# A fused transformer tower on one core: the token chain's last norm applied on ScalarE instead of VectorE

## The chip, the core and the metric

One core of a Trainium2 chip runs the whole program. The metric is the device time in microseconds of one execution; lower is better. Five engines work from queues of their own, each in program order, and wait for each other through semaphores: TensorE (PE, its weight loads shown as PEld), VectorE (DVE), ScalarE (ACT), GpSimd (POOL) and SyncE (SP, which only issues transfers).

## What is computed

The input `x` holds 64 images of 128 tokens by 64 x 3 values. Three blocks follow one another; cut to what matters:

```python
# tokens: three convolutions over a (token, column) grid with layer norms between
h = relu(conv1(layernorm(x)))
h = relu(conv2(layernorm(h)))
h = relu(conv3(layernorm(h)))            # 2 x 128 channels
res = concat(h[:, :128], h[:, 128:])     # rows of 2J = 128 values
res = layernorm(res, ln1_g, ln1_b)       # the norm of this change
h = res @ out_w + out_b
# attention with L1 distances, 8 heads of 64 values, both directions
n = layernorm(h)
a[s, t] = softmax(-sum_w |q[s, w] - k[t, w]| / 8)   # with one zero logit more
h = h + n + (gated a @ vf + a' @ vb) @ fanin_w + fanin_b
# an expert of 32 for each row
h = h + relu(relu(layernorm(h) @ W1[i]) @ W2[i])
```

A layer norm is `(x - mean) * rstd`, then a gain and a bias. For `res`, gain and bias are applied later, when the transposed rows are copied (L613), so the norm of this change is only `(x - mean) * rstd`.

## The kernel before

**Pairs and slots.** Images go in pairs: 32 pairs, `iteration(i)` for each. An iteration has 128 slots (`SLOTS`). Each slot has one `unit`: TensorE makes, with 4 matmuls at L387, the differences q - k of one head, 16 query tokens and all 128 keys, in one of three places of `psU` (slot modulo 3). Then either VectorE sums their absolute values (L788, called D units here, 71 of 128 slots) or ScalarE takes the absolute values (L587, A units, the 57 slots that `shared` names). A units are summed further by GpSimd: a transfer that adds one half to the other (`first_add`, L1045), two additions (`tree`, L1056 and L1060), and last VectorE (`last_adds`, L799, 17 slots after the group's end). TensorE may fill a place only after the unit three slots earlier was read.

**The work between the units.** Around the units each engine runs the rest of the tower at slots written out by hand: attention of the second image of the pair before, the experts of the pair before, the norm of the next pair, and the token chain `tok` of pair i + 2. `TOK_AT` gives the chain's slots: copy 3, norm a 9, conv1 20 to 42, norm b 43, conv2 53 to 65, norm c 67, conv3 75 to 109, norm d 110, transpose `turn` 121, `out` 126. `gap` = 7: a norm's statistics are taken at its slot, the norm is applied 7 slots on. A slot's extra work stands behind that slot's unit in an engine's queue.

**The last norm (d).** Slot 109: ScalarE's two ReLUs (L609). Slot 110: VectorE takes the statistics `std` and `mvd` (L813, L818), GpSimd computes `ved` = variance + eps (L1072) and `rstdd` = `ved` to the power -1/2 (L1074) in `root`, behind its `first_add` of slot 110. Slot 117: VectorE waits for `rstdd` and writes `resn` for both images (L861, two instructions), behind D unit 117. Slot 121: TensorE waits for it and transposes (L427). Slot 122: ScalarE copies with gain and bias (L613).

Around slot 117 the units are: A 115, D 116, D 117, A 118, D 119, A 120, D 121, A 122, D 123, A 124, D 125 to 127. TensorE has the attention's 16 matmuls at L486 in slots 113 to 119. Slots 119 to 122 also hold `last_adds` of slot 102 (L799), the sum L891, ScalarE's `o_half` (L707) and `th` (L712), and the gate L896.

The other norms that ScalarE applies (`norm` at L624, `experts` at L718) already use the form of the change: a scale `rstd` and a bias `nmr` = -mean x rstd, which GpSimd makes in `shift` (L1079 and L1081). Semaphore counts of each engine follow the lists of names `TOK_PE`, `TOK_ACT`, `TOK_DVE`, `TOK_POOL`.

Before the iterations, a prologue runs the token chains of pairs 0 and 1 with no units beside them; the last two iterations have no token chain. So 30 of 32 chains run beside units.

Of the kernel before, what the change touches and what calls it, by code (L numbers as in the profile page):

```python
# [21 lines left out]
ALU = mybir.AluOpType  # L22
ACT = mybir.ActivationFunctionType
AX = mybir.AxisListType

T = 128
J = 64
# [54 lines left out]


TOK_PE = Steps("conv1 conv2 conv3 turn out")
TOK_ACT = Steps("copy relu1 relu2 relu3a relu3b turned")
LN = "stat{0}0 stat{0}1 wait{0} aggr{0}0 aggr{0}1 "
LN_APPLY = "gain{0}0 gain{0}1 shift{0}0 shift{0}1 "
TOK_DVE = Steps("".join(LN.format(x) + LN_APPLY.format(x) for x in "abc") + LN.format("d") + "norm0 norm1 h")
TOK_POOL = Steps("vara rstda varb rstdb varc rstdc vard rstdd")

NORM_DVE = Steps("stat0 stat1 wait aggr0 aggr1")
NORM_POOL = Steps("var rstd mean shift hx")
# [24 lines left out]
def spread(slot, at, length, count):  # L117
# [14 lines left out]
TOK_AT = dict(copy=3, a=9, conv1=20, len1=22, b=43, conv2=53, len2=12, c=67, conv3=75, len3=34, d=110, turn=121,  # L132
              out=126, root=0, gap=7)


def vit_tower(nc, a, out):
# [4 lines left out]
    with ExitStack() as ctx:  # L141
        def sb(name, shape, dt=F32):
            return ctx.enter_context(nc.sbuf_tensor(name, shape, dt))
# [39 lines left out]
        resn = sb("resn", [T, 2, 2 * J])  # L183
        resT = sb("resT", [T, 2, T])
        st = {k: sb("st" + k, [T, 2, 6]) for k in "abcdne"}
        mv = {k: sb("mv" + k, [T, 2, 2]) for k in "abcdne"}
        ve = {k: sb("ve" + k, [T, 2]) for k in "abcdne"}
        rstd = {k: sb("rstd" + k, [T, 2]) for k in "abcdne"}
        mr = {k: sb("mr" + k, [T, 2]) for k in "ne"}
        nmr = {k: sb("nmr" + k, [T, 2]) for k in "ne"}  # L190
        h = sb("h", [T, 2, LAT])

        x1 = sb("x1", [T, 2, LAT])
# [40 lines left out]
        psC = ctx.enter_context(nc.psum_tensor("psC", [T, 512], F32))  # L234
# [116 lines left out]
        def _(pe):  # L351
# [39 lines left out]
            def tok(p, slot):  # L391
                for n in spread(slot, TOK_AT["conv1"], TOK_AT["len1"], 15):
                    dy, m = n // 3, n % 3
                    dx, o, w0, wn = ((1, 0, 0, 3), (0, 1, 0, 2), (2, 0, 1, 2))[m]
                    if n == 0:
                        pe.wait_ge(tok_dve, TOK_DVE.after(p, "shifta1"))
                        if not (isinstance(p, int) and p == 0):
                            pe.wait_ge(tok_dve, TOK_DVE.after(p - 1, "h"))
                    o_v = psC[:, 0:6 * J].rearrange("p (b j w) -> p b j w", b=2, w=3)
                    mm = nc.tensor.matmul(o_v[:, :, :, o:o + wn], w1[:, 3 * dy + dx, :],  # L400
                                          c1in[:, :, dy:dy + J, w0:w0 + wn], start=(n == 0), stop=(n == 14))
                    if n == 14:
                        mm.then_inc(tok_pe, 1)
                for n in spread(slot, TOK_AT["conv2"], TOK_AT["len2"], 10):
                    if n == 0:
                                                pe.wait_ge(tok_dve, TOK_DVE.after(p, "shiftb1"))
                    dy, dx = n // 2, n % 2
                    mm = nc.tensor.matmul(psC[:, 0:4 * J].rearrange("p (b j w) -> p b j w", b=2, w=2),  # L408
                                          w2[:, n, :], c2in[:, :, dy:dy + J, dx:dx + 2],
                                          start=(n == 0), stop=(n == 9))  # L410
                    if n == 9:
                        mm.then_inc(tok_pe, 1)
                for n in spread(slot, TOK_AT["conv3"], TOK_AT["len3"], 20):
                    if n == 0:
                        pe.wait_ge(tok_act, TOK_ACT.after(p, "relu2"))
                        pe.wait_ge(tok_dve, TOK_DVE.after(p, "shiftc1"))
                    hf, m = n // 10, n % 10
                    dy, dx = m // 2, m % 2
                    mm = nc.tensor.matmul(psC[:, 0:2 * T].rearrange("p (b a j) -> p b a j", b=2, a=2)[:, :, hf, :],  # L419
                                          w3[:, m, hf * T:hf * T + T], c3in[:, :, dy:dy + J, dx],  # L420
                                          start=(m == 0), stop=(m == 9))
                    if n == 19:
                        mm.then_inc(tok_pe, 1)
                if slot == TOK_AT["turn"]:
                    pe.wait_ge(tok_dve, TOK_DVE.after(p, "norm1"))
                    for b in range(2):
                        mm = nc.tensor.transpose(psC[:, b * T:b * T + T], resn[:, b, :], ident[:, :])  # L427
                    mm.then_inc(tok_pe, 1)
                if slot == TOK_AT["out"]:
                    pe.wait_ge(tok_act, TOK_ACT.after(p, "turned"))  # L430
                    for b in range(2):
                        mm = nc.tensor.matmul(psC[:, b * LAT:b * LAT + LAT], resT[:, b, :], wout[:, :],
                                              start=True, stop=True)
                    mm.then_inc(tok_pe, 1)
# [142 lines left out]
        def _(act):  # L577
# [12 lines left out]
            def tok(p, slot):  # L590
                if slot == TOK_AT["copy"]:
                    act.wait_ge(x_in, 16 * (p + 1))
                    if not (isinstance(p, int) and p == 0):
                        act.wait_ge(tok_dve, TOK_DVE.after(p - 1, "h"))
                    nc.scalar.activation(psC[:, 0:6 * J], xin[:, :, :].rearrange("p b f -> p (b f)"),
                                         ACT.Copy).then_inc(tok_act, 1)
                if slot == TOK_AT["conv1"] + TOK_AT["len1"]:
                    act.wait_ge(tok_pe, TOK_PE.after(p, "conv1"))
                    nc.scalar.activation(psC[:, 0:6 * J], psC[:, 0:6 * J], ACT.Relu,
                                         bias=b1[:, 0:1]).then_inc(tok_act, 1)  # L600
                if slot == TOK_AT["conv2"] + TOK_AT["len2"]:
                    act.wait_ge(tok_pe, TOK_PE.after(p, "conv2"))
                    nc.scalar.activation(psC[:, 0:4 * J], psC[:, 0:4 * J], ACT.Relu,
                                         bias=b2[:, 0:1]).then_inc(tok_act, 1)
                if slot == TOK_AT["conv3"] + TOK_AT["len3"]:
                    act.wait_ge(tok_pe, TOK_PE.after(p, "conv3"))
                    for hf in range(2):
                        y = psC[:, 0:2 * T].rearrange("p (b a j) -> p b a j", b=2, a=2)[:, :, hf, :]
                        nc.scalar.activation(y, y, ACT.Relu, bias=b3[:, hf:hf + 1]).then_inc(tok_act, 1)  # L609
                if slot == TOK_AT["turn"] + 1:  # L610
                    act.wait_ge(tok_pe, TOK_PE.after(p, "turn"))

                    nc.scalar.activation(resT[:, :, :], psC[:, 0:2 * T].rearrange("p (b t) -> p b t", b=2),  # L613
                                         ACT.Identity, bias=ln1b_col[:, 0:1], scale=ln1g_col[:, 0:1])\
                        .then_inc(tok_act, 1)
# [163 lines left out]
        def _(dve):  # L779
# [54 lines left out]
            def tok(p, slot):  # L834
# [3 lines left out]
                def rows(n):  # L838
                    return psC[:, 0:2 * n].rearrange("p (b f) -> p b f", b=2)
# [15 lines left out]
                if slot == TOK_AT["d"]:  # L855
                    dve.wait_ge(tok_act, TOK_ACT.after(p, "relu3b"))
                    stats(rows(2 * J), "d", tok_dve, after("d"))
                if slot == TOK_AT["d"] + TOK_AT["gap"]:
                    dve.wait_ge(tok_pool, TOK_POOL.after(p, "rstdd"))
                    for b in range(2):  # L860
                        nc.vector.tensor_scalar(resn[:, b, :], rows(2 * J)[:, b, :], mv["d"][:, b, 0:1],  # L861
                                                rstd["d"][:, b:b + 1], ALU.subtract, ALU.mult).then_inc(tok_dve, 1)
                if slot == TOK_AT["out"] + 1:
                    dve.wait_ge(tok_pe, TOK_PE.after(p, "out"))
                    if not (isinstance(p, int) and p == 0):
# [170 lines left out]
        def _(pool):  # L1036
# [39 lines left out]
            def shift(name, pool_sem, done):  # L1076

                pool.wait_ge(pool_sem, done("rstd"))
                nc.gpsimd.tensor_tensor(mr[name][:, :], mv[name][:, :, 0], rstd[name][:, :], ALU.mult).then_inc(pool_sem, 1)  # L1079
                pool.wait_ge(pool_sem, done("mean"))  # L1080
                nc.gpsimd.tensor_tensor(nmr[name][:, :], mr[name][:, :], minus[:, :], ALU.mult).then_inc(pool_sem, 1)  # L1081

            def tok(p, slot):
                for name in "abcd":
                    if slot == TOK_AT[name] + TOK_AT["root"]:
                        root(name, tok_dve, TOK_DVE.after(p, f"aggr{name}1"), tok_pool,
                             lambda s: TOK_POOL.after(p, s + name))

            def norm(p, slot):
                def done(s):  # L1090
# [123 lines left out]
```

## Time and profile before

| | us |
|---|---|
| median of 3 runs | 3646.7 (3644.56 to 3649.15) |
| the profiled execution, its own time | 3643.14 |
| its span, first to last instruction | 3641.3 |
| TensorE / weight loads busy | 3261.5 (90%) / 2460.2 (68%) |
| VectorE busy | 3320.0 (91%) |
| ScalarE busy | 2621.0 (72%) |
| GpSimd busy | 2435.1 (67%) |
| granted TensorE clock, mean | 0.973 of full |

Busy shares are means over the whole span; they say which engines are candidates for the bound. What limits a stretch is read from the idle times and what ended them (in square brackets behind an instruction). Start times are microseconds from the start of the span, so the same instruction in two successive iterations gives the length of a period. A granted clock of 1.00 is 2.4 GHz, 0.50 is 1.2 GHz.

### The profile page before, as it was taken

Reading aid. Unit: us, or ns where it says so; the run is one execution under the profiler, and the core shown is the slowest. Engines: PE = TensorE matmul, PEld = TensorE weight load, DVE = VectorE, ACT = ScalarE, POOL = GpSimd, SP = SyncE. Lnnn points to the kernel's source line nnn. Section 1 sums busy time; section 2 is a strip of 40 time slices with the busy share of each in tenths; the row PEclk is TensorE's granted clock in tenths of the full one; section 3 lists DMA queues with packets and bytes.
Section 4 is the critical chain, followed back from the end, with each engine's and each line's share of the span. In section 5 each row is a group of like instructions: output and inputs, shape, how many; then the busy total and the mean of one; then the engine's idle time right before and its main releaser. Section 6 shows DMA issues by size and latency. Waiting matters only on the chain. (4 is left out here: it accounts for less than half of the span.)

```text
span 3641.3 us, 77565 instructions
## 1 busy us (share of the span) xinstructions
PE 3261.5 (90%) x23008; PEld 2460.2 (68%) x23008; DVE 3320.0 (91%) x4557; ACT 2621.0 (72%) x4705; POOL 2435.1 (67%) x2212
## 2 busy tenths in 40 slices
PE   5899999999999999999999999999999999999886
PEld 4667667666677666677666677666677666677554
DVE  4899999999999999999999999999999999999885
ACT  1677777777777777777777777777777777777774
POOL 1676667676766766766766676766666766666764
PEclk8999999999999999999999999999999999999998
DMA  1677777777777777777777777777777777777774
GB/s 56 133 156 148 142 144 149 142 150 148 140 145 148 141 157 146 141 144 149 143 151 146 142 142 151 146 147 145 146 142 146 153 145 146 145 144 139 156 143 84
DMA packets 192483, 516.99 MB, mean 142 GB/s; under 512 B 67990, under 2 KB 126230, under 8 KB 151352
## 3 DMA queue, kind: packets, MB, share of 16 engines
q0 software_dynamic: 73728, 478.18, 66.7%
q1 hardware_dynamic: 118712, 38.26, 5.3%
q8 instruction: 24, 0.39, 0.0%
q14 instruction: 19, 0.16, 0.0%
HBM read 10.79 MB, written 2.10 MB: 4 GB/s over the span
## 5 line engine op out<-in xcount | busy, mean ns | idle before, releaser
L788 DVE TENSOR_REDUCE S<-psU 128x16 f32<-128x1024 f32 x2272 | 2699.7, 1215 | 190.2 <-PE psU L387 169.1
L387 PE MATMUL psU<-flat,kT 99*128 99x256 bf16 x16384 | 2304.7, 276 | 233.5 <-DVE S L788 205.2
L587 ACT ACTIVATE absd<-psU 128x1024 f32<-128x1024 f32 x1824 | 1863.9, 1024 | 612.3 <-PE psU L387 589.2
L387 PEld LDWEIGHTS psU<-flat,kT 99*128 99x128 bf16 x16384 | 1508.8, 98 | 871.1 <-DVE S L788 389.3
L1056 POOL TENSOR_TENSOR absd<-absd 128x1024 f32<-128x1024 f32 (+2 forms) x512 | 1111.3, 2171 | 307.5 <-DMA absd<-absd 304.4
L1045 POOL DMA_DIRECT2D absd<-absd x512 | 456.4, 891 | 640.5 <-ACT absd L587 571.0
L1060 POOL TENSOR_TENSOR absd<-absd 128x512 f32<-128x512 f32 (+2 forms) x512 | 586.0, 1145 | 40.1
L400 PE MATMUL psC<-c1in,w 128*128 128x256 f32 (+1 forms) x960 | 347.4, 449 | 21.3 <-DVE c1in L830 21.2
L799 DVE TENSOR_REDUCE S<-absd 128x64 f32<-128x512 f32 (+2 forms) x512 | 315.7, 617 | 7.6 <-POOL absd L1060 7.6
L486 PE MATMUL psZ<-P,v 128*128 128x256 f32 x1024 | 301.3, 387 | 0.8 <-ACT P L701 0.8
L419 PE MATMUL psC<-c3in,w 128*128 128x128 f32 x1280 | 256.2, 286 | 23.1 <-DVE c3in L830 23.1
L419 PEld LDWEIGHTS psC<-c3in,w 128*128 128x128 f32 x1280 | 195.2, 193 | 45.7 <-issue 20.2
L408 PE MATMUL psC<-c2in,w 128*128 128x256 f32 x640 | 193.0, 388 | 13.6 <-DVE c2in L830 13.6
L697 ACT ACTIVATE P<-P,rden 128x128 f32<-128x128 f32 x512 | 190.4, 401 | 0.3 <-DVE rden L888 0.3
L400 PEld LDWEIGHTS psC<-c1in,w 128*128 128x128 f32 x960 | 159.3, 205 | 36.2 <-issue 17.0
L486 PEld LDWEIGHTS psZ<-P,v 128*128 128x128 f32 x1024 | 161.5, 192 | 21.9 <-ACT P L701 12.8
L692 ACT ACTIVATE P<-S 128x129 f32<-128x129 f32 x512 | 153.3, 303 | 7.1 <-DVE S L799 6.3
L470 PE MATMUL psZ<-wqv,x1T_late 65*128 65x256 f32 x512 | 132.9, 382 | 0.7 <-ACT v L684 0.7
L408 PEld LDWEIGHTS psC<-c2in,w 128*128 128x128 f32 x640 | 102.0, 193 | 21.0 <-issue 9.8
L479 PE MATMUL psZ<-ident,P 128*128 128x128 f32 x512 | 81.3, 281 | 31.2 <-ACT P L701 20.1
L1115 POOL TENSOR_TENSOR qparts<-qrest,qparts 128x512 bf16<-128x512 f32 x64 | 83.5, 1304 | 34.2 <-ACT qparts L677 34.2
L692 ACT ACTIVATION_READ_ACCUMULATOR P<-S 128x1 f32 x512 | 98.2, 192 | 0.0
(139 smaller groups left out, 2076.1 us busy)
## 6 DMA issues: line engine op xcount, KB each, us to landing
absd<-absd POOLq DMA_DIRECT2D x320, 1024.0 KB, 7.7
absd<-absd POOLq DMA_DIRECT2D x160, 768.0 KB, 6.4
flat<-qparts SPq DMA_DIRECT2D x3072, 8.0 KB, 3.7
absd<-absd POOLq DMA_DIRECT2D x32, 512.0 KB, 4.8
xin<-in_x SPq DMA_DIRECT2D x32, 192.0 KB, 7.0
out_h<-result SPq DMA_DIRECT2D x32, 64.0 KB, 5.7
w<-in_w SPq DMA_DIRECT2D x1, 1280.0 KB
w<-in_w SPq DMA_DIRECT2D x1, 960.0 KB, 5.2
```

What stands on the lines that cost most here:

```text
L387: mm = nc.tensor.matmul(psU[:, slot % PLACES, m], kT[0:ROWS + 3, b, m, :], flat[0:ROWS + 3, half % HALVES, :, lo:lo + BLOCK], start=True, ...
L400: mm = nc.tensor.matmul(o_v[:, :, :, o:o + wn], w1[:, 3 * dy + dx, :], c1in[:, :, dy:dy + J, w0:w0 + wn], start=(n == 0), stop=(n == 14))
L408: mm = nc.tensor.matmul(psC[:, 0:4 * J].rearrange("p (b j w) -> p b j w", b=2, w=2), w2[:, n, :], c2in[:, :, dy:dy + J, dx:dx + 2], start= ...
L419: mm = nc.tensor.matmul(psC[:, 0:2 * T].rearrange("p (b a j) -> p b a j", b=2, a=2)[:, :, hf, :], w3[:, m, hf * T:hf * T + T], c3in[:, :, ...
L486: mm = nc.tensor.matmul(psZ[:, 0:2 * T], v[:, n, :, :].rearrange("p a w -> p (a w)"), P[:, n, :, :].rearrange("p a t -> p (a t)"), start=( ...
L587: nc.scalar.activation(absd[:, c % GROUPS, :, u], psU[:, slot % PLACES].rearrange("p (n a) s w -> p n (a s w)", n=2), ACT.Abs).then_inc(a_ ...
L692: nc.scalar.activation(P[:, n, :, :].rearrange("p a t -> p (a t)")[:, 0:T + 1], S[:, b, n, :], ACT.Exp, scale=-1.0 / 8.0, accum_out=den[:, ...
L788: nc.vector.tensor_reduce(S[:, b, hd, SB * c:SB * c + SB], psU[:, slot % PLACES].rearrange("p a s w -> p s a w"), AX.XY, ALU.add, apply_ab ...
L799: nc.vector.tensor_reduce(S[:, b, heads[0]:heads[-1] + 1:heads[1] - heads[0], SB * c:SB * c + SB], absd[:, c % GROUPS, 0, 0:len(heads), 0: ...
L1045: nc.gpsimd.dma_start(absd[:, c % GROUPS, 0, 0:n], absd[:, c % GROUPS, 1, 0:n], accum_op=ALU.add) \
L1056: nc.gpsimd.tensor_tensor(lo, lo, hi, ALU.add).then_inc(a_tree, 1)
L1060: nc.gpsimd.tensor_tensor(lo, lo, hi, ALU.add).then_inc(a_tree, 1)
```

## The change

ScalarE computes `resn` = `rstdd` x value + `nmrd` with two ACTIVATE instructions (Identity) at slot 117, where VectorE did it with two TENSOR_SCALAR instructions. GpSimd makes `mrd` and `nmrd` with two more small instructions, right behind `rstdd` at slot 110. ScalarE waits for GpSimd's `shiftd`; TensorE's transpose at slot 121 waits for ScalarE. No slot is changed.

```diff
-TOK_ACT = Steps("copy relu1 relu2 relu3a relu3b turned")
+TOK_ACT = Steps("copy relu1 relu2 relu3a relu3b norm0 norm1 turned")
...
-TOK_DVE = Steps("".join(LN.format(x) + LN_APPLY.format(x) for x in "abc") + LN.format("d") + "norm0 norm1 h")
-TOK_POOL = Steps("vara rstda varb rstdb varc rstdc vard rstdd")
+TOK_DVE = Steps("".join(LN.format(x) + LN_APPLY.format(x) for x in "abc") + LN.format("d") + "h")
+TOK_POOL = Steps("vara rstda varb rstdb varc rstdc vard rstdd meand shiftd")
...
-        mr = {k: sb("mr" + k, [T, 2]) for k in "ne"}
-        nmr = {k: sb("nmr" + k, [T, 2]) for k in "ne"}
+        mr = {k: sb("mr" + k, [T, 2]) for k in "dne"}
+        nmr = {k: sb("nmr" + k, [T, 2]) for k in "dne"}
...
                 if slot == TOK_AT["turn"]:
-                    pe.wait_ge(tok_dve, TOK_DVE.after(p, "norm1"))
+                    pe.wait_ge(tok_act, TOK_ACT.after(p, "norm1"))
...
+                if slot == TOK_AT["d"] + TOK_AT["gap"]:
+                    act.wait_ge(tok_pool, TOK_POOL.after(p, "shiftd"))
+                    for b in range(2):
+                        nc.scalar.activation(resn[:, b, :], psC[:, b * 2 * J:(b + 1) * 2 * J], ACT.Identity,
+                                             bias=nmr["d"][:, b:b + 1], scale=rstd["d"][:, b:b + 1]).then_inc(tok_act, 1)
                 if slot == TOK_AT["turn"] + 1:
...
-                if slot == TOK_AT["d"] + TOK_AT["gap"]:
-                    dve.wait_ge(tok_pool, TOK_POOL.after(p, "rstdd"))
-                    for b in range(2):
-                        nc.vector.tensor_scalar(resn[:, b, :], rows(2 * J)[:, b, :], mv["d"][:, b, 0:1],
-                                                rstd["d"][:, b:b + 1], ALU.subtract, ALU.mult).then_inc(tok_dve, 1)
...
                         root(name, tok_dve, TOK_DVE.after(p, f"aggr{name}1"), tok_pool,
                              lambda s: TOK_POOL.after(p, s + name))
+                        if name == "d":
+                            shift("d", tok_pool, lambda s: TOK_POOL.after(p, s + "d"))
```

## Rows read from the trace of the kernel before

**Rows 1.** The page, part 1: busy time and share of each engine.

```profile
PE 3261.5 (90%) x23008; PEld 2460.2 (68%) x23008; DVE 3320.0 (91%) x4557; ACT 2621.0 (72%) x4705; POOL 2435.1 (67%) x2212
```

**Rows 2.** Waits: who waited for whom, us in total, times, longest.

```profile
PE psU L387 <- DVE S L788: 205.2, 383, 1.3
DVE S L788 <- PE psU L387: 169.1, 306, 2.8
```

**Rows 3.** Groups by line: busy us, mean ns | idle before, releaser.

```profile
L861 DVE TENSOR_SCALAR resn<-psC,mvd,rstdd 128x128 f32<-128x128 f32 x64 | 23.1, 402 | 2.2 <-POOL rstdd L1074 2.2
...
L718 ACT ACTIVATE x<-h,nmre,rstde 128x64 f32<-128x64 f32 x64 | 24.7, 432 | 10.3 <-POOL nmre L1081 10.3
...
L609 ACT ACTIVATE psC<-psC,b 128x128 f32<-128x128 f32 x64 | 19.5, 355 | 11.4 <-PE psC L419 11.4
...
L1079 POOL TENSOR_TENSOR mre<-mve,rstde 128x2 f32<-128x2 f32 x32 | 6.3, 197 | 2.5
```

**Rows 4.** Timeline, slots 110 to 124 of one iteration: start, us, instruction, [idle before].

```profile
1613.42 0.71 POOL L1074 TENSOR_TENSOR rstdd<-ved,half 128x2 f32<-128x2 f32 x1
...
1614.85 2.36 POOL L1056 TENSOR_TENSOR absd<-absd 128x1024 f32<-128x1024 f32 x1 [0.72 <-DMA absd<-absd]
...
1617.28 1.27 POOL L1060 TENSOR_TENSOR absd<-absd 128x512 f32<-128x512 f32 x1
1617.36 1.02 ACT L587 ACTIVATE absd<-psU 128x1024 f32<-128x1024 f32 x1 [1.59 <-PE psU L387]
...
1617.59 0.60 PE L387 MATMUL psU<-flat,kT 99*128 99x256 bf16 x4
...
1617.89 0.72 DVE L861 TENSOR_SCALAR resn<-psC,mvd,rstdd 128x128 f32<-128x128 f32 x2
...
1618.52 1.22 DVE L788 TENSOR_REDUCE S<-psU 128x16 f32<-128x1024 f32 x1
...
1621.71 1.05 PE L387 MATMUL psU<-flat,kT 99*128 99x256 bf16 x8 [0.84 <-DVE S L788]
```

**Rows 5.** Timeline, a D unit that starts as TensorE ends.

```profile
1535.80 0.60 PE L387 MATMUL psU<-flat,kT 99*128 99x256 bf16 x4
...
1536.44 1.23 DVE L788 TENSOR_REDUCE S<-psU 128x16 f32<-128x1024 f32 x1 [1.28 <-PE psU L387]
```

**Rows 6.** Timeline, VectorE: starts of L861 in seven iterations.

```profile
412.75 0.40 DVE L861 TENSOR_SCALAR resn<-psC,mvd,rstdd 128x128 f32<-128x128 f32 x1
...
1508.64 0.72 DVE L861 TENSOR_SCALAR resn<-psC,mvd,rstdd 128x128 f32<-128x128 f32 x2
...
1728.70 0.72 DVE L861 TENSOR_SCALAR resn<-psC,mvd,rstdd 128x128 f32<-128x128 f32 x2
...
1838.76 0.72 DVE L861 TENSOR_SCALAR resn<-psC,mvd,rstdd 128x128 f32<-128x128 f32 x2
...
1948.41 0.72 DVE L861 TENSOR_SCALAR resn<-psC,mvd,rstdd 128x128 f32<-128x128 f32 x2
...
2057.89 0.72 DVE L861 TENSOR_SCALAR resn<-psC,mvd,rstdd 128x128 f32<-128x128 f32 x2
...
3374.75 0.40 DVE L861 TENSOR_SCALAR resn<-psC,mvd,rstdd 128x128 f32<-128x128 f32 x1
```

**Rows 7.** Windows, TensorE: stretch, length, busy (instructions), granted clock, DMA share, GB/s.

```profile
304.05:412.75 108.70, 99.25 (x721) 1.00 0.75 147
...
1531.27:1534.67 3.40, 3.02 (x11) 0.50 0.98 195
1640.49:1647.29 6.80, 6.38 (x25) 0.50 0.97 189
1753.13:1756.53 3.40, 3.40 (x12) 0.50 1.09 193
1862.36:1865.76 3.40, 3.38 (x14) 0.50 1.06 195
1971.59:1974.99 3.40, 3.40 (x14) 0.50 1.24 231
```

## The prediction

> **What bounds the kernel now.** I read the engines' shares first: TensorE 90% and VectorE 91% are the candidates, ScalarE (72%) and GpSimd (67%) are not [rows 1]. The waits then show that neither of the two is the bound throughout: TensorE waited 205.2 us at its units for VectorE, VectorE 169.1 us for TensorE [rows 2]. They take turns, and what an instruction is worth depends on whose turn it is where it stands. So I went to the timeline around slot 117. There L861 starts at 1617.89 in VectorE's queue, and D unit 119 starts behind it at 1618.52 with no idle time before it; TensorE started unit 119 at 1617.59 and took 0.60 us, so its product was there at 1618.19 [rows 4]. Before this point TensorE is the busy one (the attention's matmuls stand between the units, and ScalarE idled 1.59 us before A unit 118 until TensorE came). After it VectorE is: TensorE's unit 124 idled 0.84 us for D unit 121 [rows 4]. The change thus takes an instruction out just where the bound passes from TensorE to VectorE.
>
> The third view is the period, from the starts of L861. The first period beside units that I use is 304.05 to 412.75, 108.70 us, and the granted clock is 1.00 in all of it [rows 7]. From 412.75 to 3374.75 there are 27 periods in 2962.0 us, 109.70 on average [rows 6]. The other periods are longer because each has a stretch at 1.2 GHz, a dip of 3.4 us, or now and then one of 6.8 us (1640.49) [rows 7]. The dips keep a spacing of their own: 1753.13, 1862.36 and 1971.59 lie 109.23 apart [rows 7], while the periods they lie in last 110.06, 109.65 and 109.48 [rows 6]. So a dip slides through the iteration, and the period's length follows the distance from the start of L861 to the dip:
>
> - 24.43 us (1753.13 less 1728.70): 110.06 us
> - 23.60 (1862.36 less 1838.76): 109.65
> - 23.18 (1971.59 less 1948.41): 109.48
> - 22.63 (1531.27 less 1508.64): 109.25 (to 1617.89)
> - 22.60 (1640.49 less 1617.89): the long dip, 110.81 (to 1728.70) [rows 4, 6, 7]
>
> This is a cycle of seven periods, and it repeats: as long as the period exceeds 109.23 the distance shrinks, by ever smaller steps, until a long dip comes, after which it is 24.43 again. The Trainium skill ("TensorE: Matmul & The Clock Gate", Part 1) says that the monitor behind the gate runs freely and is not started anew by a kernel. The trace agrees: starts 109.23 us apart in periods of other lengths.
>
> **The change, part by part.**
>
> *VectorE loses L861.* Two instructions of 402 ns [rows 3]; the pair takes 0.72 us, and the next one starts 0.63 us behind its start [rows 4], so at most 0.63 us a period. But D unit 119 can't start before its product. Where VectorE had waited, it started 0.04 us after TensorE's end (1535.80 + 0.60 = 1536.40, start 1536.44) [rows 5]. So D unit 119 would start at 1618.19 + 0.04 = 1618.23 or so instead of 1618.52: **0.28 us earlier**. The bounds are 0 (another chain takes over before the end of the stretch) and 0.63 (TensorE too comes earlier); I take 0.28, which both rows give directly. Behind it, `last_adds`, L891 and D unit 121 stand without idle time, TensorE's unit 124 waits for D 121, and all move with it. L861 looks the same in all 29 later iterations that I saw (the unit behind it starts 0.63 to 0.64 us after it).
>
> *ScalarE gains two ACTIVATEs.* The trace has none from PSUM with scale and bias by pointer. Nearest: L609, same shape and source, bias alone, 355 ns; L718, scale and bias, half the columns, 432 ns [rows 3]. The pair then takes 0.6 to 0.95 us; I take 0.8, nearer L718, because of the second pointer. It stands behind A unit 115 and before A unit 118, where ScalarE idles 1.59 us [rows 4]. It ends 0.8 us before A unit 118 may start: cost 0, hidden by the wait for TensorE. Without that cover it would cost all of 0.8 x 30 = 24 us. The Trainium skill ("ScalarE: Activation LUTs", What ACT_TABLE_LOAD costs) prices a pointer operand at about 93 ns over 186 ns + 0.833 ns a column, so 479 ns for this form; a pair at 0.96 fits too, and the sum would not change.
>
> *The new wait.* ScalarE waits for `shiftd`, and A unit 118 is queued behind it. GpSimd ends `rstdd` at 1614.13 [rows 4]; two multiplications of 197 ns [rows 3] and 0.07 us before each end near 1614.67. ScalarE arrives at 1617.36 - 1.59 = 1615.77, so it doesn't wait; there are 1.1 us left. TensorE's transpose stands behind unit 121, after 1619, and `resn` would be ready by 1616.6: earlier than now.
>
> *GpSimd gains 0.53 us a period* (2 x 197 ns and the gaps). Behind `rstdd` stands `tree`, which idled 0.72 us for its transfer in this iteration [rows 4]; in others as little as nothing, so `tree` can be up to 0.53 us later there. Its result is wanted by `last_adds` behind D unit 119, some 0.9 us after it ends (1617.28 + 1.27 = 1618.55 against 1618.52 + 1.22 - 0.28 = 1619.46 with the unit moved) [rows 4]. I cost it at 0. No transfer is moved or issued anew; SP's queue is untouched.
>
> *The two chains of the prologue* have no units beside them. There VectorE waited for `rstdd` (2.2 us, all idle time of L861) [rows 3], so the chain is exposed: + 0.53 for GpSimd, 0.8 - 0.72 for the pair, twice, **+ 1.2 us**. Bounds 0 (hidden) and 1.5.
>
> *The clock.* Without dips the period becomes 108.70 - 0.28 = 108.42. Dips add what they added at the same distance. The period equals the dips' spacing when the addition is 109.23 - 108.42 = 0.81, that is where it was 109.51 before: between 23.18 (109.48) and 23.60 (109.65), near 23.25. There the distance no longer changes. It is a stable place: at a larger distance the period is longer, so the next distance is smaller, and the other way round. And it is 0.65 us away from 22.60, where the long dips came. So I expect the period to **settle at 109.23** and the long dips to vanish. This holds for any gain between about 0.1 and 1 us: the clock turns it into the same length.
>
> *The sum.* 27 x (109.23 - 109.70) = - 12.7; the two periods ahead, without a dip, - 0.28 each, - 0.6; prologue + 1.2. Together **- 12.1 us**. The profiled execution took 3643.14 (span 3641.3), which gives 3631.0; the median of the runs is 3.6 above it, outside that execution's own time because of where the dips fell, I suppose. Against the median, 3646.7 - 12.1 = **3634.6**.
>
> **Rivals.**
>
> *A. The gain adds up, the cycle of dips stays.* 29 x 0.28 = 8.1 less 1.2: - 6.9, 3639.8. For it: I know the dips from one execution, and a place at 23.25 is between two seen. Against: the spacing of 109.23 showed in every dip I looked at, and its fixed place follows from rows.
>
> *B. Nothing arrives.* A TensorE-bound chain further down takes the 0.28 us, or GpSimd's delay does. + 1.2 from the prologue: 3648. For it: TensorE and VectorE are 1% apart [rows 1]. Against: the stretch behind D unit 119 is VectorE's.
>
> *C. The whole 0.63 us.* The Trainium skill ("Perfetto Trace Analysis", Identifying the Most-Contended Engine) says the engine with the highest occupancy comes first; by that, work off VectorE counts in full. From rows it would be 29 x 0.63 = 18.3 less 1.2: 3629.6. Against: unit 119 is not ready before 1618.19, and the dips would again hold the period at 109.23.
>
> *D. Slower: the long dips come more often.* Place: the stretch some 19 to 27 us behind slot 117. TensorE's work there starts 0.28 us earlier against the dips, and if the distance where a long one is set off lies higher than 22.60, at 23.2 or above, the period falls into it again and again. With every second dip long, the mean is (110.81 + 110.06) / 2 - 0.28 = 110.16, + 0.46 x 27 = + 12.4, with the prologue + 13.6: 3660. Against: at 23.18 and 23.60 the dips were of 3.4 us.
>
> **How the numbers follow.** About 0.2% (7 us) can be told from no change. Chances: my forecast 0.55, A 0.20, B 0.11, C 0.05, D 0.09. Faster by over 0.2% (below 3639.4): forecast, C, and a third of A, 0.67. Within 0.2%: the rest of A, and B, 0.24. Slower: D, 0.09. The range leaves out B and D, 0.20 together: 3627 (the forecast with a free prologue and some periods more at 108.42, each worth 0.8) to 3644 (A with half its gain). The forecast's own range is 3629 to 3638.
>
> **What would show it.** L861 gone from VectorE; D unit 119 idle for a moment with TensorE as releaser; ScalarE's pair of 0.8 us before A unit 118, whose idle time falls from 1.59 to about 0.8; no new wait for GpSimd of weight; periods of 109.23 in a long row, no dip of 6.8 us, distances near 23.25 (counted from 0.63 us before D unit 119). Periods of 110.8 still coming every seventh would make me wrong on the clock (A); a D unit 119 that waits for GpSimd's sums, or an A unit 118 with no idle time left, wrong on what covers the added work.

## The result, and the profile after

The changed kernel takes **3633.8 us** (median of 5 runs, 3629.8 to 3634.8) against 3646.7 (3644.56 to 3649.15): ratio 0.9964, 95% interval 0.9953 to 0.9975. The forecast was 3634.6. The profiled execution took 3631.15 us, its span is 3629.3 against 3641.3: 12.0 us less.

The page's engine line and three groups of the changed kernel (busy us, mean ns | idle before, releaser):

```profile
PE 3260.4 (90%) x23008; PEld 2460.6 (68%) x23008; DVE 3300.7 (91%) x4493; ACT 2640.8 (73%) x4769; POOL 2448.3 (67%) x2276
...
L613 ACT ACTIVATE resn<-psC,nmrd,rstdd 128x128 f32<-128x128 f32 x64 | 25.6, 455 | 5.4 <-POOL nmrd L1081 5.4
...
L1079 POOL TENSOR_TENSOR mrd<-mvd,rstdd 128x2 f32<-128x2 f32 x32 | 6.2, 195 | 2.5
```

VectorE's share is 91% as before [rows 1]; neither share tells of the gain. The new ACTIVATE takes 455 ns, 23 ns over the nearer of the two rows that I had for it [rows 3]. An estimate from the figures of the Trainium skill ("ScalarE: Activation LUTs", What ACT_TABLE_LOAD costs) is 479 ns, 24 more than measured. The idle time before the new ACTIVATE (5.4 us, 3 times) is almost all in the prologue; the third time is 0.28 us at 2381.8, in the middle of the kernel. Now the waits (who for whom: us, times, longest):

```profile
PE psU L387 <- DVE S L793: 194.3, 382, 1.3
DVE S L793 <- PE psU L387: 174.8, 333, 2.2
```

They have moved a little from TensorE's side to VectorE's [rows 2]: VectorE waits 6 us more, TensorE 11 us less. The timeline of the stretch of [rows 4] (start, us, instruction, [idle before]):

```profile
1615.63 0.20 POOL L1081 TENSOR_TENSOR nmrd<-mrd,minus 128x2 f32<-128x2 f32 x1
...
1615.78 2.35 POOL L1056 TENSOR_TENSOR absd<-absd 128x1024 f32<-128x1024 f32 x1
1615.89 1.02 ACT L587 ACTIVATE absd<-psU 128x1024 f32<-128x1024 f32 x1 [1.68 <-PE psU L387]
...
1616.81 0.80 ACT L613 ACTIVATE resn<-psC,nmrd,rstdd 128x128 f32<-128x128 f32 x2
...
1618.51 1.02 ACT L587 ACTIVATE absd<-psU 128x1024 f32<-128x1024 f32 x1 [0.90 <-PE psU L387]
...
1618.74 0.60 PE L387 MATMUL psU<-flat,kT 99*128 99x256 bf16 x4
...
1619.38 1.23 DVE L793 TENSOR_REDUCE S<-psU 128x16 f32<-128x1024 f32 x1 [0.26 <-PE psU L387]
...
1622.58 1.05 PE L387 MATMUL psU<-flat,kT 99*128 99x256 bf16 x8 [0.56 <-DVE S L793]
```

Read from the top. GpSimd ended `shiftd` at 1615.83; ScalarE came to it at 1616.8, so there was no wait. Its pair took 0.80 us inside the idle time before A unit 118, which fell from 1.59 [rows 4] to 0.90; the unit itself is where TensorE lets it be. D unit 119 (1619.38) starts 0.04 us after TensorE's unit 119 ended (1618.74 + 0.60 = 1619.34), after 0.26 us of waiting: VectorE was free before its product was there. That wait, and the 0.08 us by which the records of neighbouring instructions overlap when there is no wait, are the rest of L861's 0.63 us. TensorE's unit 124 waits 0.56 us for VectorE in place of 0.84: the 0.28 us arrived there.

The periods, from the starts of `h` (L867, slot 127, an instruction that both kernels have):

```profile
426.26 0.27 DVE L867 TENSOR_TENSOR h<-psC,bout 128x128 f32<-128x128 f32 x1
...
1627.76 0.27 DVE L867 TENSOR_TENSOR h<-psC,bout 128x128 f32<-128x128 f32 x1
...
1736.99 0.27 DVE L867 TENSOR_TENSOR h<-psC,bout 128x128 f32<-128x128 f32 x1
...
3375.39 0.27 DVE L867 TENSOR_TENSOR h<-psC,bout 128x128 f32<-128x128 f32 x1
```

27 periods in 2949.13 us, **109.23 each** (109.70 before [rows 6]), and 23 of the 27 within 0.02 us of it. Before, only those ahead of a long dip came near (109.25 to 109.28). The dips of the changed kernel, two of them 7 x 109.23 = 764.6 us apart, and the stretch ahead of the first (window, length, TensorE busy, granted clock, DMA share, GB/s):

```profile
1642.22:1645.62 3.40, 3.40 (x14) 0.50 1.23 233
2406.81:2410.21 3.40, 3.40 (x14) 0.50 1.25 234
1638.70:1642.10 3.40, 1.92 (x15) 1.00 0.91 181
```

From 222 us to the last start of `h` there is a dip of 3.4 us in every period and none of 6.8 us. The engine had been busy 1.92 of 3.40 us ahead of the dip.

### The profile page after: what moved, and what is told of

Read it like the earlier page. It is cut to its first block and busy times, and to the rows that moved or that the text cites. A ratio compares the mean times of both kernels' runs of the same rounds, so it can differ in the third digit from the quotient of the medians.

```text
span 3629.3 us, 77687 instructions
## 1 busy us (share of the span) xinstructions
PE 3260.4 (90%) x23008; PEld 2460.6 (68%) x23008; DVE 3300.7 (91%) x4493; ACT 2640.8 (73%) x4769; POOL 2448.3 (67%) x2276
## 5 line engine op out<-in xcount | busy, mean ns | idle before, releaser
L486 PEld LDWEIGHTS psZ<-P,v 128*128 128x128 f32 x1024 | 161.5, 192 | 21.8 <-ACT P L706 12.7
```

Source lines behind the costliest of these rows:

```text
L486: mm = nc.tensor.matmul(psZ[:, 0:2 * T], v[:, n, :, :].rearrange("p a w -> p (a w)"), P[:, n, :, :].rearrange("p a t -> p (a t)"), start=( ...
```

## The experiments

Each kernel was timed beside the kernel before on the same chip. "Period" is the mean over the stretch between two starts of `h` that is named.

**e6: everything the change adds, nothing removed.** ScalarE's pair writes a spare tile, VectorE computes `resn` as before, behind ScalarE's pair, and TensorE waits for VectorE again.

```diff
-                        nc.scalar.activation(resn[:, b, :], psC[:, b * 2 * J:(b + 1) * 2 * J], ACT.Identity,
+                        nc.scalar.activation(spare[:, b, :], psC[:, b * 2 * J:(b + 1) * 2 * J], ACT.Identity,
...
+                if slot == TOK_AT["d"] + TOK_AT["gap"]:
+                    dve.wait_ge(tok_act, TOK_ACT.after(p, "norm1"))
+                    for b in range(2):
+                        nc.vector.tensor_scalar(resn[:, b, :], rows(2 * J)[:, b, :], mv["d"][:, b, 0:1],
+                                                rstd["d"][:, b:b + 1], ALU.subtract, ALU.mult).then_inc(tok_dve, 1)
```

> The changed kernel, but ScalarE's pair writes a tile that nobody reads, and VectorE computes resn at slot 117 with the two instructions of before, behind ScalarE's pair. So all that the change adds is there and nothing is removed. My theory: D unit 119 starts as late as before, the cycle of seven periods with a long dip is back, mean period 109.7, time 3646 to 3650. Rival (what GpSimd and ScalarE got slows the units): over 3653. If it stays at 3637, as with the stand-in of 0.52 us in e1, then it is not VectorE's time at slot 117 that decides.

Measured: 3648.56 us (3644.55 to 3652.05, 10 runs), ratio to before 1.0005 (0.9995 to 1.0014). The cycle of periods with a long dip is back, as four starts of `h` in e6 show:

```profile
539.19 0.27 DVE L873 TENSOR_TENSOR h<-psC,bout 128x128 f32<-128x128 f32 x1
650.01 0.27 DVE L873 TENSOR_TENSOR h<-psC,bout 128x128 f32<-128x128 f32 x1
1307.18 0.27 DVE L873 TENSOR_TENSOR h<-psC,bout 128x128 f32<-128x128 f32 x1
1418.01 0.27 DVE L873 TENSOR_TENSOR h<-psC,bout 128x128 f32<-128x128 f32 x1
```

A window of it, with the columns as above:

```profile
1320.80:1327.60 6.80, 6.41 (x25) 0.50 0.90 181
```

Seven periods from 539.19 to 1307.18 make 767.99, 109.71 each; the ones with a long dip take 110.82 (the four long dips of this execution lie 7, 8 and 7 periods apart, in the kernel before 8, 7 and 7). So ScalarE's and GpSimd's added work costs nothing beside units, and the whole effect is the removal from VectorE. D unit 119 stands 0.64 us after the start of the pair again, and A unit 118's idle time is 0.90 as in the changed kernel.

**e1: a stand-in of 0.52 us on VectorE.** Two unneeded sums at slot 117.

```diff
+                if slot == TOK_AT["d"] + TOK_AT["gap"]:
+                    for b in range(2):
+                        nc.vector.tensor_reduce(spare[:, b:b + 1], ln0g[:, :], AX.X, ALU.add)
```

> The changed kernel with two unneeded sums of 192 columns on VectorE at slot 117, where L861 stood, so that D unit 119 starts about 0.6 us later again (the added work of ScalarE and GpSimd stays). My theory (D unit 119's start is what the change moved, and the clock's dips turn it into a period): the cycle of seven periods with a dip of 6.8 us is back, mean period 109.7, time 3645 to 3649. Rival (the time comes from ScalarE's or GpSimd's part, or from where the code lies): stays near 3634.

Measured: 3637.45 us (3634.4 to 3642.47, 6 runs), ratio 0.9971 (0.9958 to 0.9983): a miss. VectorE's timeline, at slot 117 of one iteration, shows why:

```profile
1622.31 0.60 DVE L866 TENSOR_REDUCE spare<-ln0g 128x1 f32<-128x192 f32 x2
1622.83 1.22 DVE L794 TENSOR_REDUCE S<-psU 128x16 f32<-128x1024 f32 x1
```

D unit 119 starts 0.52 us after the pair, not 0.63, so 0.11 us of the gain was left: the stand-in was too short to be the experiment that I had meant, and e6 took its place. From `h` at 429.73 to 2286.56 there are 17 periods of 109.23; then one period was late (109.41; in it ScalarE waited 0.29 us for `nmrd`, see "What covers the added work" below), a dip of 6.8 us came at 2409.6, and the rest follows the old path (110.71, 109.95, 109.65 ...). A gain of 0.11 us stands at the edge: in this execution the period was held until one disturbance came.

**e2: one image only.**

```diff
                 if slot == TOK_AT["d"] + TOK_AT["gap"]:
                     act.wait_ge(tok_pool, TOK_POOL.after(p, "shiftd"))
-                    for b in range(2):
+                    for b in range(1):
...
+                if slot == TOK_AT["d"] + TOK_AT["gap"]:
+                    dve.wait_ge(tok_act, TOK_ACT.after(p, "norm0"))
+                    for b in range(1, 2):
+                        nc.vector.tensor_scalar(resn[:, b, :], rows(2 * J)[:, b, :], mv["d"][:, b, 0:1],
+                                                rstd["d"][:, b:b + 1], ALU.subtract, ALU.mult).then_inc(tok_dve, 1)
```

> Only the first image's norm moves to ScalarE; VectorE keeps the second (0.32 us, behind D unit 117). My theory: VectorE is free at 1618.2 in the times of before, just when TensorE's unit 119 is there, so D unit 119 starts as early as in the changed kernel, periods of 109.23, 3632 to 3636. Rival (VectorE's load counts in full): half of the gain, 3640.

Measured: 3630.51 us (3628.8 to 3634.36, 4 runs), ratio 0.9952 (0.9936 to 0.9969). The timeline of VectorE, and TensorE's unit 119:

```profile
1614.52 2.36 DVE L794 TENSOR_REDUCE S<-psU 128x16 f32<-128x1024 f32 x2
...
1616.50 0.60 PE L387 MATMUL psU<-flat,kT 99*128 99x256 bf16 x4
...
1616.79 0.40 DVE L867 TENSOR_SCALAR resn<-psC,mvd,rstdd 128x128 f32<-128x128 f32 x1
1617.14 1.23 DVE L794 TENSOR_REDUCE S<-psU 128x16 f32<-128x1024 f32 x1
```

VectorE keeps half the work and the gain is whole: D unit 119 starts 0.04 us after TensorE's unit 119 ended (1616.50 + 0.60 = 1617.10), as in the changed kernel, and the instruction that is left fits into the time in which VectorE would wait for it. What sets the gain at this place is TensorE's time, not VectorE's load. The periods of 109.22 that follow could not show this, because the dips hold the length for other gains too. But this execution has one period beside units without a dip:

```profile
206.69 0.27 DVE L873 TENSOR_TENSOR h<-psC,bout 128x128 f32<-128x128 f32 x1
315.06 0.27 DVE L873 TENSOR_TENSOR h<-psC,bout 128x128 f32<-128x128 f32 x1
```

It took 108.37 us. The same period took 109.04 in the kernel before, also without a dip, and 108.36 with the whole change (e4 below).

**e3: more off VectorE.** The changed kernel without L891, so the two halves of the attention's output are not added.

```diff
-                    nc.vector.tensor_tensor(psZ[0:LAT, 0:T], psZ[0:LAT, 0:T], o_half[0:LAT, :], ALU.add) \
-                        .then_inc(at_dve, 1)
+                    dve.sem_inc(at_dve, 1)
```

> The changed kernel without the sum of the two halves of the attention's output (L891), two instructions a period, one of them right behind D unit 119, where it takes 0.20 us of VectorE. The theory that the period is held at the dips' spacing: 109.23 again, 3631 to 3636, no gain; the distance from slot 117 to the dip goes from 23.5 to 24 us or more. Rival (the dips only add a fixed cost, each saving counts): 0.2 to 0.4 us in each of 29 periods, 3622 to 3628.

Measured: 3627.93 us (3624.27 to 3629.57, 4 runs), ratio 0.9939 (0.9922 to 0.9956). Two starts of `h`, six periods apart:

```profile
1406.96 0.28 DVE L867 TENSOR_TENSOR h<-psC,bout 128x128 f32<-128x128 f32 x1
2062.32 0.27 DVE L867 TENSOR_TENSOR h<-psC,bout 128x128 f32<-128x128 f32 x1
```

And two windows, the fourth and the fifth of the five dips between them:

```profile
1857.14:1860.54 3.40, 3.20 (x14) 0.50 1.05 195
1966.37:1973.17 6.80, 6.56 (x26) 0.50 0.87 177
```

The time lies on the edge of the rival's range (3622 to 3628), some 3 us below the lower end of mine; the periods decide between the two. The mean period was forecast well and the way there was not. Six periods from 1406.96 to 2062.32 make 655.36, 109.23 each, but they are not alike: 108.15, 108.98, 109.10, 109.16, 109.19, then 110.78 with a long dip. From the third to the last start of `h` it is 3166.3 us against 3167.6 in the changed kernel; if each saving counted, it would be some 6 us less, not 1.3. The two profiled spans differ by 2.1 us (3627.2 against 3629.3), and why the medians differ by 5.9 was not found.

**e4: fill TensorE's idle time ahead of the dip.** Ten matmuls into a free bank of PSUM, result unused. They go into these pieces of idle time, as the changed kernel has them ahead of the dip at 1642.2:

```profile
1640.64 0.61 PE L387 MATMUL psU<-flat,kT 99*128 99x256 bf16 x4 [0.70 <-DVE S L793]
1641.77 1.50 PE L387 MATMUL psU<-flat,kT 99*128 99x256 bf16 x8 [0.52 <-DVE S L793]
```

The edit:

```diff
+FILL = {17: 6, 18: 4}
...
+            def fill(slot):
+                count = FILL.get(slot, 0)
+                if count:
+                    pe.wait_ge(*bank[0])
+                for n in range(count):
+                    nc.tensor.matmul(psZ[:, 0:SB * BLOCK], kT[0:ROWS + 3, 0, 0, :], flat[0:ROWS + 3, 0, :, 0:BLOCK],
+                                     start=True, stop=True)
...
                     kq(i, 1, s)
+                    fill(s)
```

> The changed kernel with ten more matmuls (result unused) in TensorE's idle time at slots 17 and 18, just ahead of the place of the dip: 6 behind unit 17, 4 behind unit 18. If the idle time there sets off the dip, the granted clock stays at 1.00 through the iterations, periods are 108.4 (108.70 of the period without a dip, less 0.28) and the time is 3634 - 29 x 0.8 = 3611. If the dips come whatever TensorE does there, or the added matmuls delay the units: 3634 or more.

Measured: **3609.46 us** (3606.65 to 3609.64, 4 runs), ratio 0.9889 (0.9872 to 0.9905). TensorE's timeline at slots 17 and 18:

```profile
1517.98 0.61 PE L388 MATMUL psU<-flat,kT 99*128 99x256 bf16 x4 [0.26 <-ACT absd L597]
1518.43 0.82 PE L543 MATMUL psZ<-flat,kT 99*128 99x256 bf16 x6
1519.30 0.61 PE L388 MATMUL psU<-flat,kT 99*128 99x256 bf16 x4
1519.74 0.60 PE L543 MATMUL psZ<-flat,kT 99*128 99x256 bf16 x4
```

One window over 20 periods:

```profile
206.24:2373.75 2167.51, 2006.76 (x14578) 1.00 0.73 148
```

Two starts of `h`:

```profile
314.60 0.27 DVE L877 TENSOR_TENSOR h<-psC,bout 128x128 f32<-128x128 f32 x1
2264.83 0.28 DVE L877 TENSOR_TENSOR h<-psC,bout 128x128 f32<-128x128 f32 x1
```

18 periods in 1950.23 us, 108.35 each. The dips are gone from these periods (one of 10.2 us comes later, at 2370): what TensorE does ahead of them sets them off, and they cost 109.23 - 108.35 = 0.88 us a period in the changed kernel. The matmuls themselves neither cost nor bring anything beyond that: the dip-free period of e2, which has none of them, is as long (108.37).

**e5: the same ten matmuls in the kernel before.** The `fill` of e4 on the kernel before, with L861 on VectorE:

```diff
+FILL = {17: 6, 18: 4}
```

> The kernel before with the same ten added matmuls at slots 17 and 18. No dips in the iterations; then the period shows what the kernel before takes at full clock, 108.70, and the time is e4's 3609.5 + 29 x (108.70 - 108.35) - 1.3 for the prologue = 3618. The rival that the added matmuls help only where L861 is gone (that the change and the clock's dips are one effect): over 3630.

Measured: 3619.0 us (3617.49 to 3620.39, 4 runs), ratio 0.9927 (0.991 to 0.9943). Two starts of `h`:

```profile
427.01 0.27 DVE L877 TENSOR_TENSOR h<-psC,bout 128x128 f32<-128x128 f32 x1
3362.15 0.27 DVE L877 TENSOR_TENSOR h<-psC,bout 128x128 f32<-128x128 f32 x1
```

27 periods in 2935.14 us, 108.71 each. That is the length of the dip-free period of the kernel before in [rows 7], 108.70. At full clock the change is worth 108.71 - 108.35 = **0.36 us** a period, where the two kernels with dips differ by 0.47. So the dips add 0.11 us a period to the gain: they cost 0.99 us a period before and 0.88 after.

**e7: e3 with the ten matmuls.** L891 left out and the `fill` of e4:

```diff
+FILL = {17: 6, 18: 4}
...
-                    nc.vector.tensor_tensor(psZ[0:LAT, 0:T], psZ[0:LAT, 0:T], o_half[0:LAT, :], ALU.add) \
-                        .then_inc(at_dve, 1)
+                    dve.sem_inc(at_dve, 1)
```

> e3 (without L891) with the ten added matmuls. Without dips nothing holds the period, so what L891 takes counts: e3's period without a dip was 108.15, against 108.35 in e4: 29 x 0.20 = 5.8 and up to 1 at the end, 3603, where the same removal changed the mean period of the changed kernel from 109.23 to 109.18 only. Rival: nothing, 3609.5.

Measured: 3593.85 us (3591.96 to 3599.13, 4 runs), ratio 0.9861 (0.9844 to 0.9877). Two starts of `h`:

```profile
316.14 0.27 DVE L877 TENSOR_TENSOR h<-psC,bout 128x128 f32<-128x128 f32 x1
2262.54 0.27 DVE L877 TENSOR_TENSOR h<-psC,bout 128x128 f32<-128x128 f32 x1
```

18 periods of 108.13. The same removal that left the mean period at 109.23 with dips takes 0.22 us off each without them. The whole time fell by 15.6 us, 9 more than I expected: 6.9 us are there at the last start of `h` (3344.24 against 3351.16), 8 come behind it, where e4 has two dips of 13.7 us (by the granted clock) and e7 none of these. Why is open.

**e8: the matmuls elsewhere**, in idle time 16 to 19 us ahead of the dip, with both operands from `kT`. Against e4:

```diff
-FILL = {17: 6, 18: 4}
+FILL = {125: 4, 127: 6}
```

> The changed kernel with ten added matmuls at slots 125 and 127 (4 and 6), in other idle time of TensorE, some 20 us ahead of the place of the dip. If the idle time just ahead of the dip sets it off, nothing changes: a dip of 3.4 us in each period, periods of 109.23, 3631 to 3636. If any added work of TensorE would do: 3610.

Measured: 3630.19 us (3626.61 to 3635.02, 4 runs), ratio 0.9958 (0.9942 to 0.9975). 27 periods of 109.23, dips in all of them. Of the two places tried, only the one just ahead of the dip counts, so it is not the added work as such that removes them.

**e9 and e10: half of the matmuls**, e9 those of slot 17, e10 those of slot 18. Against e4:

```diff
-FILL = {17: 6, 18: 4}
+FILL = {17: 6}
```

```diff
-FILL = {17: 6, 18: 4}
+FILL = {18: 4}
```

> Half of e4: only the 6 added matmuls behind unit 17, not the 4 behind unit 18. How much idle time it takes is open. If the dip needs the sum of the idle times of 0.7 and 0.5 us, filling the larger is enough: periods of 108.35, 3609 to 3612. If each counts by itself, the dips stay, 3630 to 3636.

> The other half: only the 4 added matmuls behind unit 18, in the smaller idle time. I expect the dips to stay in most periods, with the mean period still 109.23 (what is saved in some is given back in others): 3628 to 3636. If the smaller one is enough: 3609 to 3612.

Measured: e9 **3605.92 us** (3603.2 to 3606.54, 4 runs), ratio 0.9886 (0.987 to 0.9903); e10 3606.28 us (3604.42 to 3609.99, 4 runs), ratio 0.9887 (0.9871 to 0.9904). Either half removes the dips: from the third start of `h` there is none until 2369 us in e9 (one of 10.2 us, as in e4; the next at 3373) and 3397 us in e10. I was wrong on e10: the smaller idle time is enough. Four matmuls a period, with the change, make a kernel 1.1% faster than the kernel before; they compute nothing.

## Why the prediction was right

**The start of D unit 119: right to 0.01 us.** Forecast 0.28 earlier, held back by TensorE's unit 119; the row after shows the wait of 0.26 us with that releaser, and from the start of A unit 115 to D unit 119 it is 3.49 us now, 3.78 before. e2 showed the bound from the other side.

**What covers the added work: right.** The pair took 0.80 us (forecast 0.8) in ScalarE's idle time, GpSimd's two instructions delayed nothing in the stretch shown, e6 came out at the time of before. In one iteration the cover failed, against the forecast of no wait with 1.1 us to spare: GpSimd's transfer was issued late, ScalarE waited 0.28 us for `nmrd` at 2382, and the period was 109.55; the next ones were 109.10, 109.13 and 109.16, on the way back to 109.23. In e4 the same iteration had ScalarE wait 0.29 us and VectorE 0.24 us for a sum of GpSimd's, and a dip of 10 us followed. The kernel before has that late issue at about the same time, 1.3 us later than in its other iterations, so the issue is not the change's. The wait is: ScalarE waited 0.28 to 0.29 us there in all ten profiled executions that have `nmrd`, and no instruction at slot 117 waited in the two without it (before, e5). The price is 0.3 us once, and in e4 and e9 a dip of 10.2 us with it.

**The clock: right in the main, and it made about a quarter of the result.** Of the 0.47 us by which the mean period fell, 0.36 is there at full clock (e5 against e4) and 0.11 comes from the dips; I had put 0.28 and 0.19. The period settled at 109.23, with no long dip in the profiled execution. The place was forecast at 23.25 us behind the start of L861; counted from 0.63 us before D unit 119 (1618.75) the dip at 1642.21 lies 23.46 behind. Nothing in the sum depends on that. I had said that a gain between 0.1 and 1 us would end at the same length. The lower end showed itself at 0.11 us (e1, held for 17 periods, then not). On the upper side e3, whose gain at full clock is 0.36 + 0.22 = 0.58 us, held the mean, but by other means than a fixed place: long dips came back there, once in six periods, 14.83 us behind the start of `h` (1966.37 - 1951.54), where the dips of the changed kernel stand 14.45 behind it. The picture of one stable place, with long dips only below a distance of 22.60, is thus too simple, and the forecast that any gain up to 1 us ends in equal periods was wrong; what sets off a long dip on the other side stays open. The cycle of the kernel before was also read too narrowly: between its long dips lie eight periods once and seven twice. That the dips come from TensorE's idle time just ahead of them is shown (e4, e5, e8, e9, e10); that they then fall on a spacing of 109.23 us of their own was seen in every execution with dips, and not tried beyond.

**A term that was mis-sized: the gain at full clock.** 0.28 forecast, 0.36 measured (e5 against e4). Laying the two timelines over each other, 0.29 us arise at D unit 119, and the other 0.07 at slot 75: there the D unit behind `noh` (L923 before) starts 0.14 us after it in e4 and 0.21 in e5, with no idle time recorded in either. No queue was changed there; the cause is open. Since the dips held the period, the sum did not feel it.

**The sum: right in total, its edges off.** 27 periods: forecast - 12.7, measured 2949.1 - 2962.0 = - 12.9. The two periods ahead of them: forecast - 0.6, measured 218.5 against 217.7, + 0.8, because this execution had dips there (at 222.3 and 331.5) and that of before had none. (Without dips, e4 against e5, the first of the two gained 0.63 us and the second 0.36; the added 0.3 of the first arises at slot 75 too.) Up to the third start of `h`: forecast + 1.2, measured 207.76 - 204.02 = + 3.7; the first start of `h` is at 56.75 against 56.76, the second at 98.16 against 96.89, + 1.3, and the remaining 2.5 lie between the second and the third, where this execution had dips at 113, 140 and 178 us. The profiled executions that share this prologue (the changed kernel, e3, e4, e7 to e10) have the second start at 98.16 to 99.48, the two with the prologue of before (before, e5) at 96.89 and 97.49: the change costs 0.7 to 2.6 us there, and the forecast 1.2 lies within. From the second to the third start the seven took 106.6 to 109.8 us, the two 107.1 and 111.8, so the 2.5 us are no sign of the change. Behind the last `h`, where nothing was changed: - 3.6, in a stretch that took 248.7 to 257.9 us in the nine executions. These errors are of the size by which executions of one kernel differ (5 us), and they cancelled: that the total came out to 0.1 us is luck.

**The rivals.** A (the cycle stays) fell: no long dip, periods of 109.23. B (nothing arrives) fell with the wait at unit 124. C, the full 0.63 us, fell with the 0.36 us at full clock, and with e2, where half of the removal brought the whole gain. The Trainium skill ("Perfetto Trace Analysis", Identifying the Most-Contended Engine) says to optimize the engine with the highest occupancy first. Here that was VectorE (91%), and 0.36 of the 0.63 us taken off it arrived. D (slower, with more long dips) fell in this kernel, though e3 shows that its mechanism, long dips at a larger distance, exists.

## What to carry to other kernels

Find whose turn it is at the instruction that you take away: the gain at that place is the distance to the product of the next engine, here 0.28 of 0.63 us, and half of the change would have brought it too. Where TensorE's granted clock dips once a period, measure the dips' own spacing: while they last, a saving can vanish into it (e7 against e3) or count for more than it is (0.47 for 0.36 here), and small savings are best compared with the dips filled. Above all look at what TensorE does just ahead of a dip: four to ten matmuls in its idle time there brought twice what this change did.

## What I had not expected of the hardware

Ten added matmuls made the kernel 24 us faster (3633.8 to 3609.5), and four made it 27.5 us faster (3606.3): the engine that is busy 90% of the span gained from work that nobody needs, put into 0.5 us of idle time ahead of a dip. And a saving on VectorE of 0.22 us a period could be invisible (109.23 against 109.23) until the clock was held at 2.4 GHz.
